# The low part of h moves from VectorE to GpSimd, behind a float32 copy by ScalarE, with a lag of two pairs

## The reference, cut to what matters

```
w1, w2 = W1[lang], W2[lang]                 # 512 x 128, 128 x 512
h       = relu(x @ w1 + b1[lang])           # 128 x 128
adapted = h @ w2 + b2[lang]                 # 128 x 512
y       = x + adapted
normed  = (y - mean(y)) * rsqrt(var(y) + 1e-5)      # over the 512 columns
out     = x + normed * gamma[lang] + beta[lang]
```

## Time and profile before

| | us |
|---|---|
| median of three runs | 325.74 |
| the profiled execution | 325.01 |
| its span (first to last instruction) | 323.3 |
| PE busy | 298.4 (92%) |
| DVE busy | 308.6 (95%) |
| ACT busy | 240.5 (74%) |
| POOL busy | 186.0 (58%) |

### The profile page before, as it was taken

One profiled execution on the slowest core, in us unless ns is written; L12 is line 12 of the kernel. 1 busy time (PEld: TensorE's weight loads), 2 busy tenths in 40 slices (PEclk: granted clock), 3 DMA queues, 4 the chain that ended last, 5 costly groups with the idle time before them and its releaser, 6 DMA issues. The chain is left out here.

```text
span 323.3 us, 8131 instructions
## 1 busy us (share of the span) xinstructions
PE 298.4 (92%) x2199; PEld 270.8 (84%) x2200; DVE 308.6 (95%) x679; ACT 240.5 (74%) x605; POOL 186.0 (58%) x217
## 2 busy tenths in 40 slices
PE   2549999999999999999999999999999999999961
PEld 2139899999999999999999999999999999999940
DVE  5878999999999999999999999999999999999996
ACT  4937678777787777877778777787777877778752
POOL 2960764566655566555665556655566555665553
PEclk9968999999999999999999999999999999999997
DMA  4999988666777667766677666776667666433324
GB/s 160 305 354 428 379 297 262 243 228 237 253 240 233 233 221 259 242 225 231 217 252 240 233 233 218 260 245 217 235 219 262 231 228 235 156 132 133 130 109 152
DMA packets 41711, 75.69 MB, mean 234 GB/s; under 512 B 2253, under 2 KB 7404, under 8 KB 41542
## 3 DMA queue, kind: packets, MB, share of 16 engines
q1 hardware_dynamic: 41571, 75.04, 68.2%
q10 hardware_dynamic: 99, 0.14, 0.2%
HBM read 41.62 MB, written 33.55 MB: 233 GB/s over the span
## 5 line engine op out<-in xcount | busy, mean ns | idle before, releaser
L295 POOL TENSOR_TENSOR x_io<-x_io,beta_all 128x512 f32<-128x512 f32 x128 | 161.5, 1284 | 0.0
L403 PE MATMUL ps_h<-w_all,x_T 128*128 x1024 | 143.2, 283 | 0.0
L403 PEld LDWEIGHTS ps_h<-w_all,x_T 128*128 128x128 f32 x1024 | 125.7, 193 | 1.5
L342 ACT ACTIVATE cut<-ps_y,row_sum 128x512 bf16<-128x512 f32 x128 | 87.9, 687 | 22.2 <-PE ps_y L430 22.2
L573 DVE SCALAR_TENSOR_TENSOR x_io<-ps_y,rstd,x_io 128x512 f32<-128x512 f32 x128 | 90.2, 747 | 2.5 <-DVE rstd L565 0.3
L320 ACT COPY x_T<-ps_T 128x512 f32<-128x512 f32 x128 | 74.0, 578 | 23.5 <-PE ps_T L395 23.4
L560 DVE SCALAR_TENSOR_TENSOR ps_y<-ps_y,mean,gamma_all 128x512 f32<-128x512 f32 x128 | 90.7, 753 | 0.7 <-ACT cut L342 0.4
L395 PE MATMUL ps_T<-identity,x_io 128*128 128x128 f32 x512 | 78.6, 277 | 10.7 <-DMA x_io<-in_x 10.7
L292 POOL TENSOR_TENSOR mean<-row_sum,over_h 128x2 f32<-128x2 f32 x64 | 13.0, 203 | 124.6 <-DVE ps_y L541 113.7
L541 DVE SCALAR_TENSOR_TENSOR ps_y<-x_io,b_all 128x512 f32<-128x512 f32 x124 | 83.0, 710 | 0.0
L395 PEld LDWEIGHTS ps_T<-identity,x_io 128*128 128x128 f32 x512 | 63.2, 143 | 20.1 <-issue 11.6
(11 more groups left out here) (60 smaller groups left out, 171.4 us busy)
## 6 DMA issues: line engine op xcount, KB each, us to landing
x_io<-in_x SPq DMA_DIRECT2D x64, 512.0 KB, 4.4
out<-x_io SPq DMA_DIRECT2D x63, 512.0 KB, 3.0
x_io<-in_L_cond_W SPq DMA_DIRECT2D x5, 512.0 KB, 7.2
w_all<-in_L_cond_W SPq DMA_DIRECT2D x5, 512.0 KB, 8.7
b_all<-in_L_cond_b SPq DMA_DIRECT2D x1, 2560.0 KB, 15.1
out<-x_io SPq DMA_DIRECT2D x2, 256.0 KB, 2.0
x_io<-in_L_cond_gamma SPq DMA_DIRECT2D x1, 60.0 KB
x_io<-in_L_cond_beta ACTq DMA_DIRECT2D x1, 60.0 KB
```

Source lines behind the costliest of these rows:

```text
L295: nc.gpsimd.tensor_tensor(x_slot(t), x_slot(t), of_lang(beta_all, langs[b]), ALU.add)\
L342: nc.scalar.activation(squares[:, t % 2, :], ps_y[t % Y_BANKS][:, :], ACT.Square, scale=-float(H), bias=stat(row_sum, t), accum_out=stat(s ...
L403: last = nc.tensor.matmul(part, x_T[:, t % 4, c, :], w1_all[:, bass.ds(lang, 1), c, :].rearrange("p o a -> p (o a)"), start=False, stop=(c ...
```

## The change

- POOL makes h_low, from a float32 copy of the turned h (`h_T`, two buffers) that ACT now makes ahead of h_high; DVE no longer does. On POOL the subtraction of a pair stands between its two beta additions.
- The second product of a pair comes two steps after its first product, not three; so do the squares on ACT.
- Both b1 matmuls of a pair stand side by side ahead of the first product's float32 ones.
- ACT's step begins with h_T and h_high and then copies both x.
- Three parts of W2 stand ahead of W1 in SP's queue (W2_AHEAD = 3), and ACT issues the beta rows ahead of the b1 rows.
- h_high and h_low have five buffers, not six; the scratch tiles of the cutting are smaller. START and EASE leave the lag at two throughout.

```diff
-H_PAIRS = 6
-FIRST = 3
+H_PAIRS = 5
+FIRST = 2
+LAST = 2
+START = 0
+EASE = 10
-W2_AHEAD = 2
+W2_AHEAD = 3
...
+    def ended(p):
+        return 0 if p < FIRST else p + 1 - max(LAST, FIRST - START - (p - FIRST) // EASE)
+    def heads(p):
+        return range(ended(p - 1), ended(p))
+    def low_with(n):
+        for p in range(FIRST, PAIRS):
+            if heads(p)[0] == n - 1:
+                return p - 1
+        return PAIRS - 1 if n == ended(PAIRS - 1) + 1 else None
...  POOL
-            def add_beta(n):
+            def low_h(p):
+                pool.wait_ge(h_T_ready, p + 1)
+                pool.wait_ge(h_high_ready, p + 1)
+                nc.gpsimd.tensor_tensor(flat(h_low[:, p % H_PAIRS, :, :]), flat(h_T[:, p % 2, :, :]),
+                                        flat(h_high[:, p % H_PAIRS, :, :]).bitcast(F32), ALU.subtract).then_inc(h_low_ready, 1)
+            def mean_and_beta(n, p):
...
                     nc.gpsimd.tensor_tensor(x_slot(t), x_slot(t), of_lang(beta_all, langs[b]), ALU.add)\
                         .then_inc(x_beta_ready, 1)
+                    if b == 0 and p is not None:
+                        low_h(p)
...
-            for n in range(PAIRS):
-                add_beta(n)
+            for p in range(FIRST - 1):
+                low_h(p)
+            mean_and_beta(0, None)
+            for n in range(1, PAIRS):
+                mean_and_beta(n, low_with(n))
...  ACT
+                if p >= 2:
+                    act.wait_ge(h_low_ready, p - 1)
+                nc.scalar.copy(flat(h_T[:, p % 2, :, :]), pair_of(ps_hT)).then_inc(h_T_ready, 1)
                 nc.scalar.copy(flat(h_high[:, p % H_PAIRS, :, :]), pair_of(ps_hT)).then_inc(h_high_ready, 1)
...
             def step(p):
+                high_h(p - 1)
                 if p < PAIRS - 1:
                     copy_x(2 * p + 2)
-                if p > 0:
-                    high_h(p - 1)
-                if p < PAIRS - 1:
                     copy_x(2 * p + 3)
                 copy_h(p)
...  PE
+            def put_b1(p):
+                for b in range(2):
+                    nc.tensor.matmul(h_sums(2 * p + b), of_lang(pick, langs[p][b]), b1_parts[:, :],
+                                     start=(b == 0), stop=False, skip_group_check=True)
...
                 if p > 0:
-                    pe.wait_ge(h_low_ready, p)
+                    pe.wait_ge(h_T_ready, p)
+                    pe.wait_ge(h_high_ready, p)
...
-                    if b == 0 and p > 0:
-                        turn_h(p - 1)
+                    if b == 0:
+                        if p > 0:
+                            turn_h(p - 1)
+                        put_b1(p)
                     first_product(2 * p + b, langs[p][b])
...  DVE
-            def low_h(p):
-                dve.wait_ge(h_high_ready, p + 1)
-                nc.vector.scalar_tensor_tensor(flat(h_low[:, p % H_PAIRS, :, :]), pair_of(ps_hT), 1.0,
-                                               flat(h_high[:, p % H_PAIRS, :, :]).bitcast(F32), ALU.mult, ALU.subtract)\
-                    .then_inc(h_low_ready, 1)
...
+            for n in range(PAIRS):
                 scale_pair(n, langs[n])
...
                 finish_pair(n)
-                if p is not None:
-                    low_h(p)
                 if n + 2 < PAIRS:
                     seed_pair(n + 2, langs[n + 2])
```

More of the change, by code:

```diff
@@ L41, in build @@
     by_dve = [n for n in range(2 * L) if n not in by_act]
-    assert FIRST + 2 <= H_PAIRS
+    assert FIRST < H_PAIRS
     with ExitStack() as ctx:
@@ L62, in build @@
         b2_all = sb("b2_all", [128, L, H], F32)
-        cut = sb("cut", [128, 3, H], BF16)
+        cut = sb("cut", [128, 2, H], BF16)
         parts = sb("parts", [128, 3 * H], BF16)
         b2_rows = sb("b2_rows", [3 * L, H], F32)
-        b2_cut = sb("b2_cut", [3 * L, 2, H], BF16)
+        pool_cut = sb("pool_cut", [3 * L, H], BF16)
         b1_rows = sb("b1_rows", [3 * L, A], F32)
@@ L85, in build @@
         h_rows = sb("h_rows", [128, 2, 2, A], F32)
+        h_T = sb("h_T", [128, 2, 2, S], F32)
         h_high = sb("h_high", [128, H_PAIRS, 2, S], F32R)
@@ L146, in build @@
         h_turned = sem("h_turned")
+        h_T_ready = sem("h_T_ready")
         h_high_ready = sem("h_high_ready")
@@ L283, in _ @@
             pool.wait_ge(s_beta_rows, 16)
-            cut_in_three(x_io[0:3 * L, 2 * ROWS_PAIR + 1, :], b2_cut[:, 0, :], parts[0:3 * L, H:2 * H], 0, beta_parts_ready)
+            cut_in_three(x_io[0:3 * L, 2 * ROWS_PAIR + 1, :], pool_cut[:, :], parts[0:3 * L, H:2 * H], 0, beta_parts_ready)
             pool.wait_ge(s_b2_rows, 16)
-            cut_in_three(b2_rows[:, :], b2_cut[:, 1, :], parts[0:3 * L, 2 * H:3 * H], 4, b2_parts_ready)
-            def add_beta(n):
+            cut_in_three(b2_rows[:, :], pool_cut[:, :], parts[0:3 * L, 2 * H:3 * H], 4, b2_parts_ready)
+            def low_h(p):
[4 more added lines that the diff above has]
+            def mean_and_beta(n, p):
                 langs = langs_of(pool, n)
@@ L308, in _ @@
             nc.scalar.activation(table_load[:, :], eps[:, :], ACT.Sqrt, bias=eps[:, 0:1])
+            act.dma_start(x_io[0:3 * L, 2 * ROWS_PAIR + 1, :],
+                          beta.unsqueeze(0).broadcast_to([3, L, H])).then_inc(s_beta_rows, 16)
             act.dma_start(b1_rows[:, :],
                           b1.unsqueeze(0).broadcast_to([3, L, A])).then_inc(s_b1_rows, 16)
-            act.dma_start(x_io[0:3 * L, 2 * ROWS_PAIR + 1, :],
-                          beta.unsqueeze(0).broadcast_to([3, L, H])).then_inc(s_beta_rows, 16)
             act.dma_start(b2_rows[:, :],
@@ L365, in _ @@
                 copy_spread(n)
-            for n in range(W2_AHEAD):
+            for n in range(2):
                 high_w2(n)
@@ L369, in _ @@
                 copy_spread(n)
+            high_w2(2)
             copy_x(2)
             copy_x(3)
-            high_w2(2)
+            high_w2(3)
             copy_h(0)
@@ L375, in _ @@
             high_h(0)
-            high_w2(3)
+            high_w2(4)
             copy_x(5)
             copy_h(1)
-            high_w2(4)
-            step(2)
             for p in range(FIRST, PAIRS):
-                square_pair(p - FIRST)
+                for n in heads(p):
+                    square_pair(n)
                 step(p)
-            square_pair(PAIRS - FIRST)
+            square_pair(ended(PAIRS - 1))
             high_h(PAIRS - 1)
-            for n in range(PAIRS - FIRST + 1, PAIRS):
+            for n in range(ended(PAIRS - 1) + 1, PAIRS):
                 square_pair(n)
@@ L397, in turn_x, with h_sums @@
                 last.then_inc(x_turned, 1)
+            def h_sums(t):
+                return pair_of(ps_h)[:, (t % 2) * A:(t % 2 + 1) * A]
+            def put_b1(p):
+                for b in range(2):
+                    nc.tensor.matmul(h_sums(2 * p + b), of_lang(pick, langs[p][b]), b1_parts[:, :],
+                                     start=(b == 0), stop=False, skip_group_check=True)
             def first_product(t, lang):
-                part = pair_of(ps_h)[:, (t % 2) * A:(t % 2 + 1) * A]
-                nc.tensor.matmul(part, of_lang(pick, lang), b1_parts[:, :], start=True, stop=False)
                 for c in range(C):
-                    last = nc.tensor.matmul(part, x_T[:, t % 4, c, :],
+                    last = nc.tensor.matmul(h_sums(t), x_T[:, t % 4, c, :],
                                             w1_all[:, bass.ds(lang, 1), c, :].rearrange("p o a -> p (o a)"),
-                                            start=False, stop=(c == C - 1))
+                                            start=False, stop=False, skip_group_check=True)
                 if t % 2 == 1:
@@ L457, in _ @@
             for p in range(PAIRS):
-                if p >= FIRST:
-                    n = p - FIRST
+                for n in heads(p):
                     if n == 0:
@@ L477, in _ @@
                         put_b2(2 * p + b, langs[p][b])
-            for n in range(PAIRS - FIRST, PAIRS):
+            for n in range(ended(PAIRS - 1), PAIRS):
                 for b in range(2):
                     second_product(2 * n + b, langs[n][b])
-                if n == PAIRS - FIRST:
+                if n == ended(PAIRS - 1):
                     turn_h(PAIRS - 1)
@@ L576, in _ @@
             dve.wait_ge(over_h_ready, 2)
-            for n in range(W2_AHEAD):
-                mean_of_w2(n)
+            mean_of_w2(0)
+            mean_of_w2(1)
             for n in by_dve:
@@ L581, in _ @@
                 nc.vector.tensor_copy(spread_to(n), spread_bank(n)).then_inc(spread_dve, 1)
-            for n in range(W2_AHEAD):
-                low_w2(n)
             mean_of_w2(2)
+            low_w2(0)
+            low_w2(1)
+            low_w2(2)
             mean_of_w2(3)
-            low_w2(2)
             mean_of_w2(4)
-            low_h(0)
             low_w2(3)
@@ L596, in _ @@
             seed_early(1)
-            low_h(1)
```

(6 more changed lines are left out.)

## The result

The changed kernel takes 339.31 us (median of 4 runs, 338.92 to 340.82), the kernel before 325.62 in the same comparison: 1.0416 times as long, 95% interval 1.038 to 1.045. The forecast was 337.9 us, slower. The profiled execution took 338.92 us with a span of 337.2.

A forecast was written before the change was run, and what follows sets the result against it. PE and DVE were both taken as full at 4.49 us a period; POOL's stretch plus seeds, 3.35 + 0.55 + 0.71 + 0.08 = 4.69, over 61 periods, with start and end, gave 337.9 us, range 326 to 350.

The forecast's parts named there:

- The loop of POOL and the seeds: Steady period: POOL's mean, additions and subtraction, 3.35 us, then the blocked seeds and the next mean, 4.69 us in all.
- Rival 1: Steady period: no blocking between seeds and POOL, PE stays the bound at 4.44 us, total 322.6 us; chance 0.16.
- The first seed's length: First seed of each pair on DVE, held by POOL's second addition: 1.0 to 1.2 us instead of 0.69.
- DVE's own floor goes from 4.49 to 4.16: DVE per period: without the low part of h its order shortens by 0.33 us.
- Both are balanced at 4.49: Steady period of the kernel before: PE and DVE both read as full at 4.49 us.
- PE idle about 0.25 per period, ended by POOL's subtraction: Sign expected in PE's steady rows if the forecast was right: about 0.25 us idle until POOL's subtraction ends.
- b1 side by side: PE's first products: adjacent b1 matmuls save 0 to 0.06 us per pair, taken as 0.05, PE's floor 4.44.
- The start: Kernel start: third W2 part ahead delays PE by 1.23 us; first W2 product at 32.9, mean of pair 2 at 39.5.
- the 335.4: Whole kernel: forecast end of the span in us, to which 1.71 outside the span was added for 337.1.
- the rows of 19.66 and 33.17: Start of the kernel before: DVE low part took 1.63 us under POOL's subtraction; POOL's addition took 1.80 instead of 1.28.
- rival 2: Steady period: DVE and POOL share in part, DVE losing 0.35 us; period 4.51, total 326.9 us; chance 0.08.
- rival 3: POOL's subtraction costs 1.00 us instead of 0.69, with blocking; 19 us more, 357 us; chance 0.04.

The follow-up runs named there:

- the split kernel: Changed kernel with the low part of h split by sample, VectorE making the first sample's and GpSimd the second's; 322.85 us, 0.991 of the kernel before.

## Why the prediction was right, step by step

- **The loop of POOL and the seeds** was the step that mattered, and it holds in each piece: POOL idle 1.34 (forecast 1.34), subtraction 0.74 and 0.68 from start to start (0.74 and 0.69), first seed ending 0.56 after POOL (0.55), period 4.71 in the rows, 4.717 on average (4.69). That it is blocking, and not POOL's amount of work, is shown: the same POOL work with a seed of one SBUF input gives 4.44. Rival 1's period of 4.44 is the one of that run, so that term was right for a machine without the blocking; its time, 322.6, is 2.4 us short of the run's 324.96, whose 61 periods alone took 1.8 more than 61 x 4.44.
- **The first seed's length** was forecast as 1.0 to 1.2 and is 1.31. VectorE arrives 2.83 us after its scale began (152.91 to 155.74), as taken (2.84), but the mean begins 0.22 after the scale, not with it; so VectorE waits longer. The seed's end, and so the period, doesn't depend on it.
- **"DVE's own floor goes from 4.49 to 4.16"** was wrong at the first number. The order that VectorE kept at 4.49 it also keeps at 4.44, in two runs. That it was "back at the same place each period" with hardly an idle time was read as a full engine; it was following PE. "Both are balanced at 4.49" should have been: PE bounds at 4.49, and VectorE has at least 0.05 to spare. It had no part in the sum, but it hid that one part of the change is a gain by itself.
- **"PE idle about 0.25 per period, ended by POOL's subtraction"**: the wait is there, but not as idle time. PE is idle 0.38 us in the 50 of the window above. What grows is the time from the start of the second sample's product with W1 to the start of the W2 product. Here it is in the changed kernel and then in the run with the low part on VectorE:

```profile
154.50 1.06 PE L443 MATMUL ps_h<-w_all,x_T 128*128 x8
155.48 0.47 PE L471 MATMUL ps_y<-w_high,h_high 128*128 x1
```

```profile
154.25 1.06 PE L430 MATMUL ps_h<-w_all,x_T 128*128 x8
155.07 0.48 PE L457 MATMUL ps_y<-w_high,h_high 128*128 x1
```

  It is 0.98 against 0.82; the median over the periods from 120 to 260 us is 1.07 against 0.81. The duration in the row, 1.06, covers the wait.
- **b1 side by side**, taken at 0.05: the two matmuls stand in 0.28 us together, and the period falls from 4.49 to 4.44. Right. In the changed kernel it should be worth nothing, as PE isn't the bound there. No run takes it out; the trace fits: PE starts the last matmul with W1 4.41 us after a W2 product, as in the run with b1 alone, and the rest of the 4.70 is the wait.
- **The start** was forecast with the first W2 product at 32.9, it came at 32.47; the mean of pair 2 at 39.5, it came at 39.38. The second agreement is luck in part: from one to the other it took 6.91, not 6.63. The seed of pair 2 already meets POOL's addition (the row of 37.62: 0.98 instead of 0.69), which this term of the forecast left out, and that nearly made up for the early product.
- **The mis-sized term** is the period: 0.027 x 61 = 1.6 us of the 1.8 by which the span came out over the 335.4. About half of it is in every period: the median from mean to mean is 4.703, not 4.69. The other half, 0.9 us, is two long periods, 5.34 from the mean of pair 4 and 4.95 from that of pair 17. In the first VectorE stands still:

```profile
51.11 0.17 DVE L601 RECIPROCAL rstd<-std 128x2 f32<-128x2 f32 x1 [1.14 <-issue]
```

  The load of language ids that VectorE has before this reciprocal is its longest, 2.04 us, and ends at 51.07. The kernel before has the same at this pair (1.44 us, and an idle time of 0.72), yet its W2 products stay 4.49 apart there. The new loop has no slack for it. In the period of 4.95 POOL's addition starts 0.20 late, put down to issue; what makes either late stays open.
- The rule of the Trainium skill's page "SBUF — State Buffer" (section "Who interferes with whom") gave the same time as the rows of 19.66 and 33.17. The trace after agrees for this pair of instructions, but for one thing: the blocked seed ends 0.56 us after POOL, a little less than the 0.69 that it takes alone. Its other half, that an instruction with at most one SBUF input (outside VectorE's 2-port modes) doesn't contend, is the run with the seed from the bank: 0.69 us beside an addition of 1.29.
- The median came out 1.4 us over the forecast: 1.8 from the span, less 0.3, as the median lies 0.39 over the profiled execution and not 0.73. The partly shared row (rival 2) and the dear subtraction (rival 3) were not seen. Rival 3's 1.00 came from the row of 2.09, which is itself lengthened: the same instruction took 1.55 at 14.43, where no VectorE instruction with two SBUF inputs ran beside it.

## What to carry to other kernels

Before work goes onto GpSimd because it is idle, ask what VectorE does in that idle time: if it is an instruction with two SBUF inputs, the idle time isn't free, and the added work comes on top of it. A loop of two engines that take turns shows no idle engine; look for an instruction that takes longer than the same instruction elsewhere, and for fewer instructions in a window. Test the parts of a change one by one: here a reordering of two matmuls was worth 0.7% alone and was buried under a loss of 4%.

## What the runs showed of the hardware

- A scalar_tensor_tensor on VectorE with two SBUF inputs that starts during a tensor_tensor on GpSimd ends 0.55 to 0.56 us after it, wherever in it it started (1.31 and 0.97 us long in two kernels, 0.69 alone). One case differs: beside a tensor_scalar on 30 partitions it took 1.09 instead of 0.74 and ended first (the row of 17.98 in the earlier trace rows). With one input from PSUM it takes 0.69 either way.
- A small instruction behind a wait on GpSimd costs less than its length: without the mean of 0.20 us the loop was 0.06 shorter.
- The load of the language ids into VectorE's registers took 524 to 2035 ns in the changed kernel's profile, with a median of 532, and 528 to 2053 in the split kernel's, with a median of 972. VectorE's wait of 1.28 us before the reciprocal at 50.94 in that profile, put down to issue, stands right behind the longest of them, and PE lost 0.86 us in that period. What makes such a load slow stays open.
